# Edge layers of a graph kernel: both one-hots of a group in one VectorE compare with two sources

## The chip, the cores and the metric

The kernel runs on one core of one Trainium2 chip. The metric is the device time of an execution in microseconds; the smaller the better. The core has a matrix engine (TensorE, PE in the profile, its weight loads PEld), VectorE (DVE), ScalarE (ACT), GpSimd (POOL) and SyncE (SP), which mostly issues DMAs. Each engine works through a list of its own and waits on semaphores for the others.

## The reference, cut to what matters

There are 12500 nodes with 128 features and 212500 edges (both directions of 100000 random pairs and a loop at each node), sorted by destination.

```python
def _edge_conv(x, src, dst, W1, b1, W2, b2, n_nodes):
    xi = x[dst]
    xj = x[src]
    m = jnp.concatenate([xi, xj - xi], axis=-1)
    h = jax.nn.relu(m @ W1 + b1) @ W2 + b2
    agg = jax.ops.segment_max(h, dst, num_segments=n_nodes)
    return jnp.where(jnp.isfinite(agg), agg, 0.0)
# three of these with relu between them, then
x = _layernorm(x + edge_layers(x))
# then a relation stage: means of messages over 8 edge types, summed through 8 weight matrices
x = _layernorm(x + relu(relation_stage(x)))
```

## The kernel before

Each of the three edge layers first makes two tables of the nodes: `table` in SBUF (x times W1's first half less its second, plus the bias, looked up by destination) and `tab_b` in DRAM (x times W1's second half, looked up by source). Then it goes over the edges in order of destination. 128 edges are a tile, 4 tiles (GT) are a group of 512 edges, and 8 groups (LG) are the body of a loop. A layer has 428 groups, the three have 1284.

A group goes through the engines like this. The inner function that does a group on each engine is named `step`:

- GpSimd (`gather_body`, L826 to L837) issues four indirect DMAs, one per tile, which fetch the rows of `tab_b` by source into `rows[k]`. It first waits for `s_p1`, which says that TensorE has done with the rows of eight groups before. The list of row numbers of each DMA lies in SBUF (`idx`).
- SyncE loads `two[k]`, the group's local destination numbers (`locs`, bf16, 0 to 255 within a block of 256 nodes, each repeated on all partitions) and the marks at which a new destination begins (`cuts`).
- VectorE (L1556 to L1596) makes the one-hots: `hot_t[s]` is 128 x 2 x 512 f32, with two halves. Half 0 has a one where an edge's local number is the lane's number, half 1 where it is that number plus 128. Two instructions make them, L1562 and L1563, each of 512 columns with one tensor and one number per lane (`pidx`, `pidx_up`). There are two such buffers; VectorE waits in front for `locs` and until TensorE has done with the buffer's former content. The second of the two raises `s_hot`.
- TensorE (L955 to L991) waits for `s_hot`, for the copied part of the table (`s_tabs`), for `s_h1` and for the four gathers (`s_rows`). It adds in PSUM the transposed rows (L966) and the products of the table's two halves with the two one-hots (L968). After that it multiplies by W2 for the group before (L975), and turns the scan's output of two groups before (L990).
- ScalarE applies the relu (L1279), copies the 4 table parts of a later group (L1270) and evicts the turned output (L1291).
- VectorE runs the segment maximum as a scan over the 512 columns (L1590), with `cuts` from SBUF and the product from PSUM as its sources. In its list it comes after the one-hots of two groups later.
- SyncE stores the result in `scan_rows`.

In layer 0 VectorE also makes small one-hots for the segments' ends (L1570 to L1584). In layer 1 it sorts the edges by source and type for the relation stage: pieces of a bitonic sort (`sort_stage`, L1651; L1669, L1670, L1674, L1675) are placed between the groups by a table of times written out by hand. In layer 2 it ranks the sorted keys (L1700 on, among them the scans of L1756 and the RECIPROCAL of L1764). GpSimd's four gathers per group are the same in all three layers. The relation stage after them has gathers of its own (L891).

Ahead of everything VectorE makes small constants (L1412 to L1424), each with a wait for the one before; `pidx` holds the lane's number, `pidx_up` the lane's number plus 128.

Of the kernel before, what the change touches and what calls it, by code (L numbers as in the profile page):

```python
# [32 lines left out]
P = 128  # L33
# [3 lines left out]
GT = 4  # L37
# [8 lines left out]
def gnn_kernel(nc, x, src, dst, etype, params, w_rel, out):  # L46
# [55 lines left out]
    with ExitStack() as ctx:  # L102
        def sb(name, shape, dt=F32):
            return ctx.enter_context(nc.sbuf_tensor(name, shape, dt))
# [9 lines left out]
        ident = sb("ident", [P, P])  # L114
        iota = sb("iota", [P, P])
        pidx = sb("pidx", [P, 1])
        pidx_up = sb("pidx_up", [P, 1])
        lane_f = sb("lane_f", [P, 1])
        ones = sb("ones", [P, 1])
        ones_b = sb("ones_b", [P, 1], BF16)  # L120
# [96 lines left out]
        locs = [v[:, 0:GT * P] for v in two]  # L217
# [13 lines left out]
        hot_t = [a.cut(2 * GT * P).rearrange("p (h e) -> p h e", h=2) for _ in range(2)]  # L231
# [207 lines left out]
        GP_PAD, GP_ALL = 3, 9  # L439
        SLOTS = LG  # L440

        PV_CONST = 13
        PV_FULL = PV_CONST + 2
        PV_WIN0 = PV_FULL + 2
        PV_START = PV_WIN0 + 4
# [734 lines left out]
        def _(act):  # L1180
# [84 lines left out]
            def copy_tables(l, g, s):  # L1265
                _, blk = nc.values_load_multi_w_load_instructions(
                    blocks[0:1, bass.ds(g * GT, GT)], engines=[ACT_ENGINE], min_val=0, max_val=NS,
                    skip_runtime_bounds_check_because=WHY)
                for t in range(GT):
                    last = a_(tabs[s][:, t, :], table[:, bass.ds(blk[t] * W2P, W2P)], ACT.Copy)  # L1270
                last.then_inc(s_tabs, 1)
# [24 lines left out]
            for l in range(3):  # L1296
                if l == 0:
                    act.wait_ge(s_pv, PV_CONST)
                    act.wait_ge(s_w, NW * 16)
# [99 lines left out]
        def _(dve):  # L1399
            v = nc.vector  # L1400
# [3 lines left out]
            def pv(ins):  # L1404

                done[0] += 1
                ins.then_inc(s_pv, 1)
                dve.wait_ge(s_pv, done[0])
                return done[0]
# [10 lines left out]
            pv(v.memset(eps[:, :], EPS))  # L1420
            pv(v.memset(zeros[:, :], 0.0))
            pv(v.tensor_scalar(lane_f[:, :], pidx[:, :], 1.0, None, ALU.add))
            pv(v.tensor_scalar(pidx_up[:, :], pidx[:, :], float(P), None, ALU.add))
            assert pv(v.memset(table[:, NB * P:], 0.0)) == PV_CONST  # L1424

            dve.wait_ge(s_last, 16)
# [129 lines left out]
            def step(l, i, k, lo=False, hi=False):  # L1556
                live = lambda d: not ((lo and k < d) or (hi and k - OV >= d))
                if live(0):
                    at = Lt(l, i, k)
                    dve.wait_ge(s_two[at.k], 16 * (at.n + 1))  # L1560
                    dve.wait_ge(s_p1, at.G - 1 + SLOTS)
                    v.tensor_scalar(hot_t[at.s][:, 0, :], locs[at.k], pidx[:, 0:1], None, ALU.is_equal)  # L1562
                    v.tensor_scalar(hot_t[at.s][:, 1, :], locs[at.k], pidx_up[:, 0:1], None, ALU.is_equal  # L1563
                                    ).then_inc(s_hot, 1)
                    if l == 0:
                        if at.j == 0:
                            dve.wait_ge(s_endc[at.h], 16 * (at.n + 1))
                            dve.wait_ge(s_found, at.G + 1)
                            tick()
                            v.tensor_scalar(end_up, end_c[at.h], float(P), -float(P), ALU.is_ge, ALU.mult  # L1570
                                            ).then_inc(s_lane, 1)
                            for f, side in enumerate((ALU.is_lt, ALU.is_ge)):
                                v.tensor_scalar(lanes[at.h][:, :, f], end_c[at.h], float(P), lane_f[:, 0:1], side, ALU.mult)
                            dve.wait_ge(s_lane, 2 * at.H + 1)
                            tick()
                            v.tensor_tensor(end_lo[at.h], end_c[at.h], end_up, ALU.add).then_inc(s_lane, 1)
                            dve.wait_ge(s_lane, 2 * at.H + 2)
                            tick()
                        dve.wait_ge(s_found, at.G + 1)
                        for t in range(GT):  # L1580
                            col = at.j * GT + t
                            last = v.tensor_scalar(ends[at.s][:, t, :], iota_b[:, :], end_lo[at.h][:, col:col + 1], None,  # L1582
                                                   ALU.is_equal)
                        last.then_inc(s_ends, 1)  # L1584
                if live(2):
                    at = Lt(l, i, k, 2)
                    dve.wait_ge(s_p2, at.G + 3)
                    dve.wait_ge(s_p3, at.G + 1)
                    dve.wait_ge(s_scan, at.G + 2)
                    v.tensor_tensor_scan(scan[at.s], cuts[at.k], ps[:, 2 + at.s, :],  # L1590
                                         scan[1 - at.s][:, GT * P - 1:GT * P], ALU.min, ALU.max).then_inc(s_scan, 1)
                    if l == 0 and at.j == HG - 1:
                        dve.wait_ge(s_found, at.G + 3)
                        tick()
                        v.tensor_copy(end_at[:, :, bass.ds((at.i * 2 + at.h) * HT, HT)],
                                      ps[:, 6 + at.h, 0:2 * HT].rearrange("p (t f) -> p f t", f=2)).then_inc(s_ecol, 1)  # L1596
# [300 lines left out]
            for l in range(3):  # L1897
# [26 lines left out]
                for k in range(LG):  # L1924
                    step(l, 0, k, lo=True)
                alone = (1, SORT_END + 1, WIN_BODY + NQ + 1)[l]
                for i in range(1, alone):
                    for k in range(LG):
                        step(l, i, k)
                        if l == 1:  # L1930
                            sort_work(i, k)
                        else:
                            rank_work(i, k)
                with loop(dve, alone, NL) as i:
                    for k in range(LG):
                        step(l, i, k)
# [163 lines left out]
```

## Time and profile before

| | us |
|---|---|
| median of 3 runs | 9618.12 (9596.58 to 9622.49) |
| profiled execution | 9607.98 |
| its span | 9606.1 |
| edge layers' gathers, first and last start | 145.4 and 7164.9 |
| GpSimd busy | 7060.4 |
| TensorE busy | 6722.9 |
| VectorE busy | 4648.1 |
| ScalarE busy | 4896.4 |

The busy time of an engine is the time in which at least one of its instructions ran. A group of instructions is the instructions of one source line and shape; a mean over it hides that a few are much longer. "Idle before" is time in which the engine had none running just ahead of such an instruction, and behind the arrow stands what ended it. Where that is "issue", nothing of another engine did. In a timeline an instruction stands with its start and its duration.

### The profile page before, as it was taken

To read this page: it belongs to the slowest core of one execution; us is meant where nothing else is said; L and a number is where in the kernel's file an instruction comes from. 1 tells how busy PE (TensorE), PEld (TensorE's weight loads), DVE (VectorE), ACT (ScalarE), POOL (GpSimd) and SP (SyncE) were. 2 spreads that over 40 slices of the span, in tenths; PEclk is the share of its full clock that TensorE was granted. 3 is DMA by queue.
4 is the path that set the end of the run, shared out by engine and by line. 5 is a ranking of instruction groups with operands and counts; after the bars stand their busy time and mean duration, and the time that the engine had idled before them with its cause. 6 is when DMAs were issued, how large, how long until landed. Compare 5 with 4: busy or idle time off the path is not lost. (4 is left out here: it accounts for less than half of the span.)

```text
span 9606.1 us, 159944 instructions
## 1 busy us (share of the span) xinstructions
PE 6722.9 (70%) x41098; PEld 5264.4 (55%) x41098; DVE 4648.1 (48%) x9610; ACT 4896.4 (51%) x11866; POOL 7060.4 (73%) x7196
## 2 busy tenths in 40 slices
PE   6777777876677777777767777778768555555555
PEld 5665656665555666566555656656653343333333
DVE  4555555555466555555435444444446333333334
ACT  2444444443344444444424444444445777777776
POOL 4777777776777777777777777777774777777775
PEclk9999999999899999999989999999999777777777
DMA  5555555654455555565545565556657222222222
GB/s 142 153 153 154 153 153 153 153 155 133 120 149 150 151 149 151 149 149 149 155 120 142 163 156 160 161 154 153 156 142 265 54 54 54 54 54 54 54 54 67
DMA packets 896156, 1259.78 MB, mean 131 GB/s; under 512 B 185847, under 2 KB 601079, under 8 KB 895270
## 3 DMA queue, kind: packets, MB, share of 16 engines
q1 hardware_dynamic: 650494, 784.23, 26.5%
q0 software_dynamic: 230048, 471.99, 21.8%
q10 hardware_dynamic: 15408, 0.88, 0.1%
q8 instruction: 121, 1.98, 0.1%
q14 instruction: 85, 0.70, 0.0%
HBM read 834.14 MB, written 424.01 MB: 131 GB/s over the span
## 5 line engine op out<-in xcount | busy, mean ns | idle before, releaser
L834 POOL DMA_INDIRECT agg<-tab_b,agg x5136 | 5109.6, 995 | 1596.4 <-issue 1523.0
L968 PE MATMUL ps<-tab_a 128*128 128x128 f32 x20544 | 3090.0, 285 | 2.8 <-issue 2.8
L968 PEld LDWEIGHTS ps<-tab_a 128*128 128x128 f32 x20544 | 2883.2, 202 | 3.5 <-issue 3.5
L1590 DVE TENSOR_TENSOR_SCAN agg<-agg,ps 128x512 f32<-128x512 bf16 x1284 | 1639.7, 1277 | 2159.3 <-PE ps L975 2158.2
L966 PE MATMUL ps<-ident,agg 128*128 128x128 f32 x5136 | 1482.7, 289 | 1701.4 <-DMA agg<-tab_b,agg 1577.7
L1279 ACT ACTIVATE agg<-ps 128x512 f32<-128x512 f32 x1284 | 766.6, 597 | 3604.2 <-PE ps L968 3596.7
L891 POOL DMA_INDIRECT work<-z_tab,work x1708 | 1611.7, 944 | 576.1 <-issue 498.3
L1163 PE MATMUL ps<-tab_a,work 128*128 128x256 f32 x3416 | 1231.5, 523 | 912.4 <-DMA work<-z_tab,work 631.1
L966 PEld LDWEIGHTS ps<-ident,agg 128*128 128x128 f32 x5136 | 754.0, 147 | 1936.0 <-issue 1349.2
L1270 ACT ACTIVATE tab_a<-tab_a 128x256 f32 x5136 | 1713.6, 404 | 50.8 <-issue 41.1
L1163 PEld LDWEIGHTS ps<-tab_a,work 128*128 128x128 f32 x3416 | 843.4, 258 | 1300.6 <-DVE tab_a L2035 1107.9
L2035 DVE TENSOR_TENSOR tab_a<-ps,tab_a 128x256 f32 x1708 | 724.3, 424 | 1417.7 <-PE ps L1163 1230.9
L975 PE MATMUL ps<-agg,w 128*128 128x512 f32 x2568 | 1345.1, 606 | 0.0
L1356 ACT ACTIVATE tab_a<-tab_a,work 128x256 f32<-128x256 f32 x1708 | 883.7, 588 | 466.5 <-PE ps L1163 452.8
L990 PEld LDWEIGHTS ps<-ident,agg 128*128 128x128 f32 x5136 | 610.4, 141 | 471.3 <-issue 466.5
L990 PE MATMUL ps<-ident,agg 128*128 128x128 f32 x5136 | 786.2, 276 | 2.4 <-DVE agg L1590 2.3
L1347 ACT ACTIVATE tab_a<-work 128x256 f32<-128x256 f32 x1708 | 727.4, 496 | 61.8 <-ACT tab_a L1356 5.7
L1291 ACT ACTIVATE agg<-ps 128x512 f32<-128x512 f32 x1284 | 738.3, 575 | 15.5 <-PE ps L990 10.6
L1582 DVE TENSOR_SCALAR agg<-iota_b,agg 128x128 bf16<-128x128 bf16 x1712 | 327.6, 280 | 688.1 <-PE ps L982 670.1
L1562 DVE TENSOR_SCALAR tab_a<-agg,pidx 128x512 f32<-128x512 bf16 x1284 | 626.3, 488 | 47.9 <-PE ps L968 45.2
L1563 DVE TENSOR_SCALAR tab_a<-agg,pidx_up 128x512 f32<-128x512 bf16 x1284 | 626.7, 488 | 0.0
L813 POOL DMA_INDIRECT work<-scan_rows,endrow x294 | 287.7, 979 | 194.2 <-issue 99.4
(251 smaller groups left out, 2978.9 us busy)
## 6 DMA issues: line engine op xcount, KB each, us to landing
agg<-row_two SPq DMA_DIRECT2D x1284, 256.0 KB
scan_rows<-agg SPq DMA_DIRECT2D x1284, 256.0 KB
agg<-tab_b,agg POOLq DMA_INDIRECT x5136
z_tab<-tab_a SPq DMA_DIRECT2D x84, 512.0 KB, 3.7
work<-z_tab,work POOLq DMA_INDIRECT x1708, 2.5
tab_b<-work SPq DMA_DIRECT2D x42, 448.0 KB, 3.1
work<-in_x SPq DMA_DIRECT2D x26, 448.0 KB, 5.3
z_tab<-work SPq DMA_DIRECT2D x14, 512.0 KB, 3.9
```

The source lines that it names most:

```text
L834: g.indirect_dma_start(rows[k][:, t, :], None, tab_b, bass.IndirectOffsetOnAxis(ap=idx[at.h][:, at.j * GT + t:at.j * GT + t + 1], axis=0)) ...
L891: g.indirect_dma_start(got[k % LG][:, t, :], None, z_tab, bass.IndirectOffsetOnAxis(ap=meta_of(k, 0, t).bitcast(I32), axis=0)).then_inc(s_ ...
L966: mm(to, rows[at.k][:, t, :], ident[:, :], is_transpose=True, start=True, stop=False)
L968: last = mm(to, tabs[at.s][:, t, h * P:(h + 1) * P], hot_t[at.s][:, h, t * P:(t + 1) * P], start=False, stop=(h == 1))
L975: mm(ps[:, 2 + at.s, :], w2[:, l], h1[at.s], start=True, stop=True).then_inc(s_p2, 1)
L990: last = tr(ps[:, 4 + at.s, t * P:(t + 1) * P], scan[at.s][:, t * P:(t + 1) * P], ident[:, :])
L1163: last = mm(flat[:, to:to + W2P], got[k % LG][:, t, :], hot_r[k % 4][:, t, :], start=True, stop=True)
L1270: last = a_(tabs[s][:, t, :], table[:, bass.ds(blk[t] * W2P, W2P)], ACT.Copy)
L1279: a_(h1[at.s], ps[:, at.s, :], ACT.Relu).then_inc(s_h1, 1)
L1291: a_(h2e[at.s], ps[:, 4 + at.s, :], ACT.Copy).then_inc(s_h2e, 1)
L1356: last = a_(hot_r[k % 4][:, t, :], off_r[k % 2][:, t, :], ACT.Relu, scale=meta_of(k, 3, t), bias=meta_of(k, 2, t))
L1590: v.tensor_tensor_scan(scan[at.s], cuts[at.k], ps[:, 2 + at.s, :], scan[1 - at.s][:, GT * P - 1:GT * P], ALU.min, ALU.max).then_inc(s_scan, 1)
```

## The change

The two compares become one. Its first source is `locs`, read twice over, its second the two columns of a new constant `pidx_two`, each number repeated over 512 columns. The destination and the condition are the same, and so are the waits and the semaphore. The constant `pidx_up` falls away, `pidx_two` takes its place, with one more small instruction among the constants.

```diff
-        pidx_up = sb("pidx_up", [P, 1])
+        pidx_two = sb("pidx_two", [P, 2])
...
-        PV_CONST = 13
+        PV_CONST = 14
...
-            pv(v.tensor_scalar(pidx_up[:, :], pidx[:, :], float(P), None, ALU.add))
+            pv(v.tensor_scalar(pidx_two[:, 1:2], pidx[:, :], float(P), None, ALU.add))
+            pv(v.tensor_copy(pidx_two[:, 0:1], pidx[:, :]))
...
-                    v.tensor_scalar(hot_t[at.s][:, 0, :], locs[at.k], pidx[:, 0:1], None, ALU.is_equal)
-                    v.tensor_scalar(hot_t[at.s][:, 1, :], locs[at.k], pidx_up[:, 0:1], None, ALU.is_equal
+                    v.tensor_tensor(hot_t[at.s], locs[at.k].unsqueeze(1).to_broadcast([P, 2, GT * P]),
+                                    pidx_two[:, :].unsqueeze(2).to_broadcast([P, 2, GT * P]), ALU.is_equal
                                     ).then_inc(s_hot, 1)
```

## Rows read from the trace of the kernel before

**Rows 1.** The page: busy us (share of the span) and instructions of each engine.
```profile
PE 6722.9 (70%) x41098; PEld 5264.4 (55%) x41098; DVE 4648.1 (48%) x9610; ACT 4896.4 (51%) x11866; POOL 7060.4 (73%) x7196
```

**Rows 2.** Waits of GpSimd: us in total, times, longest us.
```profile
POOL agg L834 <- issue: 1523.0, 4895, 16.0
...
POOL agg L834 <- PE ps L968: 51.5, 169, 0.3
```

**Rows 3.** Waits of TensorE.
```profile
PE ps L966 <- DMA agg<-tab_b,agg: 1577.7, 985, 16.8
...
PE ps L966 <- DVE tab_a L1563: 95.3, 62, 6.3
```

**Rows 4.** Waits of VectorE.
```profile
DVE agg L1590 <- PE ps L975: 2158.2, 797, 14.5
```

**Rows 5.** Groups of GpSimd, 200:2200, 3060:4660, 5300:6900 us: busy, mean ns | idle before.
```profile
L834 POOL DMA_INDIRECT agg<-tab_b,agg x1556 | 1527.0, 981 | 474.3 <-issue 451.7 <-PE ps L968 16.5 <-ACT agg L1261 6.1
...
L834 POOL DMA_INDIRECT agg<-tab_b,agg x1212 | 1232.4, 1017 | 369.4 <-issue 355.7 <-ACT agg L1261 7.3 <-PE ps L968 6.4
...
L834 POOL DMA_INDIRECT agg<-tab_b,agg x1241 | 1203.5, 970 | 378.3 <-issue 358.8 <-PE ps L968 13.7 <-ACT agg L1261 5.8
```

**Rows 6.** Instructions of line 834: ns min/median/max, first and last start us.
```profile
L834 POOL DMA_INDIRECT agg<-tab_b,agg x5136: 938/944/5210, 145.4 to 7164.9; - x198
```

**Rows 7.** Timeline of VectorE and GpSimd in layer 0: start us, us, instruction.
```profile
1502.92 0.46 DVE L1562 TENSOR_SCALAR tab_a<-agg,pidx 128x512 f32<-128x512 bf16 x1
...
1503.30 0.48 DVE L1563 TENSOR_SCALAR tab_a<-agg,pidx_up 128x512 f32<-128x512 bf16 x1
...
1503.35 1.24 POOL L834 DMA_INDIRECT agg<-tab_b,agg  x1 [0.30 <-issue]
```

**Rows 8.** Timeline in layer 1, two places of the sort.
```profile
3062.89 1.20 DVE L1674 TENSOR_TENSOR work<-work 128x1024 f32<-128x1024 f32 x1
...
3063.10 1.80 POOL L834 DMA_INDIRECT agg<-tab_b,agg  x1 [0.30 <-ACT agg L1261]
...
3073.56 1.20 DVE L1674 TENSOR_TENSOR work<-work 128x1024 f32<-128x1024 f32 x1
...
3073.97 1.61 POOL L834 DMA_INDIRECT agg<-tab_b,agg  x1 [0.30 <-issue]
```

**Rows 9.** Timeline in layer 1, a gather that began before the sort's compare.
```profile
3121.39 0.94 POOL L834 DMA_INDIRECT agg<-tab_b,agg  x1 [0.30 <-issue]
...
3121.77 1.20 DVE L1674 TENSOR_TENSOR work<-work 128x1024 f32<-128x1024 f32 x1
```

**Rows 10.** Timeline in layer 2, the RECIPROCAL and the first of the gathers that began beside it.
```profile
5189.28 12.93 DVE L1764 RECIPROCAL work<-work 128x2048 f32<-128x2048 f32 x1
...
5190.31 0.94 POOL L834 DMA_INDIRECT agg<-tab_b,agg  x1 [0.30 <-issue]
```

**Rows 11.** Timeline in layer 2, the edge scan and a scan of two SBUF sources.
```profile
5153.22 1.28 DVE L1590 TENSOR_TENSOR_SCAN agg<-agg,ps 128x512 f32<-128x512 bf16 x1 [5.99 <-PE ps L975]
...
5153.35 0.94 POOL L834 DMA_INDIRECT agg<-tab_b,agg  x1 [0.30 <-issue]
...
5154.41 4.46 DVE L1756 TENSOR_TENSOR_SCAN work<-work,ones 128x2048 f32<-128x2048 f32 x1
...
5154.60 5.17 POOL L834 DMA_INDIRECT agg<-tab_b,agg  x1 [0.30 <-issue]
```

**Rows 12.** Groups of the page, the first of the two one-hots: busy, mean ns | idle before.
```profile
L1562 DVE TENSOR_SCALAR tab_a<-agg,pidx 128x512 f32<-128x512 bf16 x1284 | 626.3, 488 | 47.9 <-PE ps L968 45.2
```

**Rows 13.** Groups of VectorE, 3060:4660 us.
```profile
L1674 DVE TENSOR_TENSOR work<-work 128x1024 f32<-128x1024 f32 x116 | 139.3, 1201 | 0.0
```

**Rows 14.** Instructions of line 1685, a product with a repeated mask: ns min/median/max.
```profile
L1685 DVE TENSOR_TENSOR work<-ps,work x28: 664/665/668, 3180.2 to 4476.7; 128x512 f32<-128x512 f32 x28
```

**Rows 15.** Timeline of VectorE among the constants.
```profile
6.78 0.15 DVE L1423 TENSOR_SCALAR pidx_up<-pidx 128x1 f32<-128x1 f32 x1
7.05 0.27 DVE L1424 MEMSET tab_a<- 128x256 f32 x1
```

## The prediction

> **What bounds the kernel now.** I read the engines' shares first. GpSimd (POOL) is the busiest at 73%, TensorE 70%, VectorE 48% [rows 1]. Three quarters of the span are edge layers, so what counts is which engine never rests there. The waits of GpSimd say it: ahead of its 5136 row gathers (L834) it waited 1523.0 us for "issue" in 4895 cases, and only 51.5 us for TensorE [rows 2]. "Issue" is time in which nothing outside held it, about 0.30 us ahead of every gather. It is simply working through its list. The other engines wait for it: TensorE 1577.7 us for the gathers' landings against 95.3 us for the one-hots [rows 3], and VectorE 2158.2 us for TensorE ahead of its scan [rows 4].
>
> The second step is whether the length of a gather is the length of a group. In layer 0, 1556 gathers fell into 2000 us, one per 1.285 us; that is the mean gather, 0.981, and 474.3 / 1556 = 0.305 of idle. In the part of layer 1 that holds the sort's long compares, 1212 fell into 1600 us, one per 1.320 us: 1.017 and 0.305 again [rows 5]. So nanoseconds added to a gather come out in the period one for one. A group is four gathers and there are 1284 groups: 0.1 us per group is 128 us of the kernel.
>
> The third step is why a gather is longer in one place than in another. Its median is 0.944 us, its longest 5.210 us [rows 6]. The timelines of GpSimd and VectorE side by side show it. A gather that began 0.05 us into the second one-hot compare took 1.24 us, not 0.94 [rows 7]. Beside the sort's TENSOR_TENSOR, which has two sources in SBUF, gathers that began 0.21 and 0.41 us into it took 1.80 and 1.61 us [rows 8]. Put e for the end of the VectorE instruction and s for the start of the gather: 0.94 + (e - s - 0.13) gives 1.24 for the first, 1.80 and 1.60 for the others. The gather needs something that VectorE holds, once, some 0.1 us after its start, and waits for it to the end of that instruction. One that is past this point isn't disturbed: at 3121.39 a gather was already 0.38 us old when the same TENSOR_TENSOR began; it took 0.94 us, and the TENSOR_TENSOR its usual 1.20 [rows 9]. What decides isn't VectorE's being busy: beside a 12.93 us RECIPROCAL (one source) the ten gathers that began kept 0.94 us; one stands here [rows 10]. Neither does the scan of L1590, whose second source lies in PSUM: the gather at 5153.35 began inside one and took 0.94 us. Beside a scan of two SBUF sources, the second a column of ones repeated 2048 times, a gather took 5.17 us [rows 11].
>
> **The change, part by part.**
>
> *The compare itself.* Removed per group: two TENSOR_SCALAR of 512 columns, 488 ns each (the second's mean is the same), 0.98 us [rows 12]. Added: one TENSOR_TENSOR of 1024 columns from SBUF to SBUF. The trace has that shape in the sort: 1201 ns for one of its two lines [rows 13]; I take 1.20 us. Two things differ from these rows. One source is bf16, and both are repeated by a step of zero. The nearest row on repeating, 512 columns with a repeated mask at 665 ns [rows 14], shows no cost. From that row's pace 1024 columns would be 1.33 us at most, and from the two compares removed at least 0.98. So VectorE is busy some 0.22 us more per group (bounds 0 and +0.35). It idles 2158.2 / 1284 = 1.68 us per group for the scan's input [rows 4], and that covers it. If this cover were gone, it would be 0.22 x 1284 = 280 us. The one-hots come ready about 0.33 us later (0.38 + 0.48 from start to end now [rows 7]); TensorE was kept by them 62 times [rows 3], so at most 62 x 0.33 = 20 us are added to its wait, in a TensorE that has over a microsecond per group to spare. I count nothing.
>
> *What it does to the gathers.* This is the term. The new instruction has two sources in SBUF, like the sort's compares and the scan with the ones, and it lasts 1.20 us in one piece. A gather starts each 0.94 + 0.30 = 1.24 us, so nearly every one-hot finds one gather at its sensitive point. If the two run free of each other, the wait per group is 1.17 x 1.17 / (2 x 1.24) = 0.55 us, with 1.17 = 1.20 - 0.03 as the stretch that is held. The trace has a dose to check this by: in the sort window a gather averaged 1017 ns, in the quieter part of layer 2 970 ns [rows 5]; 1212 x 0.047 = 57 us over 116 pairs of these compares is 0.49 us per pair. In a pair, the gather caught in the first half passes at the seam, and its successor needs its turn about 1.14 us later, near the end of the second, so a pair costs about what one does. I take 0.50. Bounds: 0.25 (the 0.49 split evenly over the pair's two instructions), and 1.17 (every one catches a gather at its very start).
>
> *What goes.* The old compares also hold gathers up. In layer 2, where little else runs on VectorE, the mean gather is 970 ns [rows 5] against the median of 944 [rows 6]: 4 x 0.026 = 0.10 us per group. Layer 0, with its other small compares, has 4 x 0.037 = 0.15. I take 0.12.
>
> *Net:* 0.50 - 0.12 = 0.38 us per group, x 1284 = 488 us. Bounds 0.13 x 1284 = +167 and 1.05 x 1284 = +1348.
>
> *Preparation.* One more tiny instruction, with its own wait, before the first layer: from L1423's start to the next instruction's is 0.27 us [rows 15]. It stands in a chain that GpSimd waits for, so +0.3 us.
>
> The Trainium skill has a rule here ("SBUF — State Buffer", section "SBUF: two separate sides"): VectorE and GpSimd share a pair of ports under an exclusive lock, which a VectorE instruction in a two-port mode takes, and one with two SBUF inputs too, against a GpSimd instruction that reads SBUF. That speaks against this change, and rows 8 and 11 agree with it. But it also says that whoever starts first keeps the pair for the whole instruction; rows 9 show otherwise for these gathers. What that would give is rival B.
>
> **Sum.** The profiled execution took 9607.98 us (span 9606.1). 9608 + 488 = 10096 us; I say 10100. The median of the runs, 9618.12, is 0.1% above the profiled one, which is within this. Layers alone change; the relation stage (L891) has none of these compares.
>
> **Rivals.**
>
> *A, the other side: the new compare does not hold the gathers.* Place: the sensitive point of L834. Its lane numbers are two values per partition, repeated, and might be held inside VectorE, as a scalar is. Then the old stalls go and nothing replaces them: -0.12 x 1284 = -154 us, 9454 us. It decides if the mean gather falls to about 945 ns. For it: the scan with its second source in PSUM is harmless. Against it: the repeated ones of rows 11 were no protection. 8%.
>
> *B, whole instructions exclude each other.* Then the compare would wait for the running gather, start with its end, and the next gather, 0.30 us later, would stand for 1.20 - 0.30 = 0.90 us in each group: +0.78 x 1284 = 1002, 10610 us. This is the skill's rule as written; rows 9 speak against it. 3%.
>
> *C, the phases fall well.* The compare starts when a scan ends, which follows from a gather's landing, so its phase is not random. If it mostly began just after a gather's sensitive point, the stall would be near the lower bound or under it: +167 us at 0.25, 9775 us; down to no change. The old compares bear on this: by the same random reckoning their two holds of about 0.45 us would cost 2 x 0.45 x 0.45 / 2.48 = 0.16, and layer 2 shows 0.10. 9%, 2% of it within no change.
>
> *D, the compare is slow.* At the pace of the two-source scan of rows 11 (4.46 us for 2048 columns) it would last 2.2 us, and hold a gather 2.2 - 0.62 = 1.6 us in each group: +1.48 x 1284 = 1900, 11510 us. 2%; no compare in the trace is that slow.
>
> **How the numbers follow.** The forecast has 78%, with its own range from 0.32 to 0.52 us net per group, 10020 to 10280 us. Below it lie A and C, above B and D and the three-in-a-row of layer 1 (sort, sort, one-hot), which can catch two gathers. For 8 in 10 I give 9950 to 10320. A difference of 0.3%, 29 us, is about what can be told from none; by that: faster 0.09, same 0.02, slower 0.89.
>
> **What would show it.** One group L1563 of TENSOR_TENSOR 128x1024 with 1284 instructions near 1200 ns; mean of L834 up from 995 to about 1090 ns (0.38 / 4), its median still near 944 in the undisturbed ones, and gathers of up to 2.1 us lying beside the compare by the formula above; the idle of GpSimd still "issue" at 0.30; TensorE's wait for landings larger; relation stage unchanged. It is wrong if L834 keeps its mean, or if the mean rises and the span doesn't.

## The result and the profile after

The changed kernel took 10176.36 us in the median of 4 runs (10153.47 to 10189.58), the kernel before 9620.31 on the same chip. The ratio is 1.0579, with a 95% interval of 1.0551 to 1.0607: slower by 5.8%. A later job gave 10173.92 against 9603.69, ratio 1.0592 (1.0574 to 1.0610). There are chips on which the kernel before takes a third longer and the sign turns; they have a section below.

The page of the changed kernel, engines and the groups that answer to [rows 1] and [rows 12]:

```profile
PE 6930.3 (68%) x41098; PEld 5462.9 (54%) x41098; DVE 5043.6 (50%) x8327; ACT 4899.5 (48%) x11866; POOL 7631.3 (75%) x7196
...
L834 POOL DMA_INDIRECT agg<-tab_b,agg x5136 | 5673.4, 1105 | 1596.0 <-issue 1566.4
...
L891 POOL DMA_INDIRECT work<-z_tab,work x1708 | 1615.7, 946 | 576.3 <-issue 499.5
...
L1563 DVE TENSOR_TENSOR tab_a<-agg,pidx_two 128x1024 f32<-128x1024 bf16 x1284 | 1547.7, 1205 | 44.2 <-PE ps L968 44.0
```

The gathers of the kernel before, whole trace:

```profile
L834 POOL DMA_INDIRECT agg<-tab_b,agg x5136 | 5109.6, 995 | 1596.4 <-issue 1523.0
```

The span grew from 9606.1 to 10180.4 us, by 574.3. The gathers' busy time grew by 5673.4 - 5109.6 = 563.8 us, and the idle time ahead of them stayed, 1596.0 against 1596.4. The relation stage's gathers (L891) gained 1615.7 - 1611.7 = 4 us. Longer gathers in the edge layers account for 98% of the loss. The compare takes 1205 ns in the mean.

The answers to [rows 3] and [rows 4], waits of TensorE and VectorE:

```profile
PE ps L966 <- DMA agg<-tab_b,agg: 1924.9, 955, 17.0
...
PE ps L966 <- DVE tab_a L1563: 107.4, 53, 8.7
```
```profile
DVE agg L1591 <- PE ps L975: 2299.2, 781, 16.9
```

TensorE waits 347 us longer for landings and 12 us longer for the one-hots. VectorE is busy 395 us longer and yet waits 141 us longer for TensorE: the other engines stand behind GpSimd. The answers to [rows 5], in layer 0, in the sort's stretch of layer 1 (3255 to 5055 us here) and in the quiet part of layer 2 (5700 to 7500):

```profile
L834 POOL DMA_INDIRECT agg<-tab_b,agg x1444 | 1560.8, 1081 | 440.3 <-issue 431.8 <-PE ps L968 4.6 <-ACT agg L1261 4.0
...
L834 POOL DMA_INDIRECT agg<-tab_b,agg x1219 | 1429.9, 1173 | 371.7 <-issue 364.7 <-ACT agg L1261 5.2 <-PE ps L968 1.8
...
L834 POOL DMA_INDIRECT agg<-tab_b,agg x1288 | 1386.2, 1076 | 392.8 <-issue 385.4 <-ACT agg L1261 4.0 <-PE ps L968 3.4
```

Per group that is 4 x (1081 - 981) = 0.40 us more in layer 0, 4 x (1173 - 1017) = 0.62 among the sort, 4 x (1076 - 970) = 0.42 in layer 2. The timeline of layer 0 has the single case, to be read like [rows 7]:

```profile
1506.13 1.20 DVE L1563 TENSOR_TENSOR tab_a<-agg,pidx_two 128x1024 f32<-128x1024 bf16 x1
1506.20 1.95 POOL L834 DMA_INDIRECT agg<-tab_b,agg  x1 [0.30 <-issue]
...
1509.24 1.21 DVE L1563 TENSOR_TENSOR tab_a<-agg,pidx_two 128x1024 f32<-128x1024 bf16 x1
1509.71 1.56 POOL L834 DMA_INDIRECT agg<-tab_b,agg  x1 [0.31 <-issue]
```

The prediction's formula, 0.94 + (e - s - 0.13), gives 1.94 and 1.55 us. It holds for the whole trace and not only here: of the gathers that start while a compare runs, between 0.03 us after its start and 0.16 us before its end, there are 1000, and all 1000 took what the formula says, within 0.07 us. Among the sort, where three two-source instructions follow each other without a pause, two gathers in a row are caught:

```profile
3269.17 1.20 DVE L1675 TENSOR_TENSOR work<-work 128x1024 f32<-128x1024 f32 x1
3269.52 1.67 POOL L834 DMA_INDIRECT agg<-tab_b,agg  x1 [0.30 <-issue]
3270.29 1.22 DVE L1676 TENSOR_TENSOR work<-work 128x1024 f32<-128x1024 f32 x1
3271.42 1.22 DVE L1563 TENSOR_TENSOR tab_a<-agg,pidx_two 128x1024 f32<-128x1024 bf16 x1
3271.49 1.97 POOL L834 DMA_INDIRECT agg<-tab_b,agg  x1 [0.30 <-issue]
```

### The profile page after: what moved, and what is told of

Read it like the earlier page. It is cut to its first block and busy times, and to the rows that moved or that the text cites. A ratio compares the mean times of both kernels' runs of the same rounds, so it can differ in the third digit from the quotient of the medians.

```text
span 10180.4 us, 158661 instructions
## 1 busy us (share of the span) xinstructions
PE 6930.3 (68%) x41098; PEld 5462.9 (54%) x41098; DVE 5043.6 (50%) x8327; ACT 4899.5 (48%) x11866; POOL 7631.3 (75%) x7196
## 5 line engine op out<-in xcount | busy, mean ns | idle before, releaser
L834 POOL DMA_INDIRECT agg<-tab_b,agg x5136 | 5673.4, 1105 | 1596.0 <-issue 1566.4
L968 PE MATMUL ps<-tab_a 128*128 128x128 f32 x20544 | 3273.4, 295 | 8.3 <-issue 8.3
L968 PEld LDWEIGHTS ps<-tab_a 128*128 128x128 f32 x20544 | 3047.4, 213 | 9.2 <-issue 9.2
L966 PE MATMUL ps<-ident,agg 128*128 128x128 f32 x5136 | 1534.0, 299 | 2051.0 <-DMA agg<-tab_b,agg 1924.9
L891 POOL DMA_INDIRECT work<-z_tab,work x1708 | 1615.7, 946 | 576.3 <-issue 499.5
L966 PEld LDWEIGHTS ps<-ident,agg 128*128 128x128 f32 x5136 | 783.4, 153 | 2279.5 <-issue 1573.8
L1563 DVE TENSOR_TENSOR tab_a<-agg,pidx_two 128x1024 f32<-128x1024 bf16 x1284 | 1547.7, 1205 | 44.2 <-PE ps L968 44.0
L975 PE MATMUL ps<-agg,w 128*128 128x512 f32 x2568 | 1374.5, 618 | 0.0
L990 PEld LDWEIGHTS ps<-ident,agg 128*128 128x128 f32 x5136 | 612.6, 142 | 483.6 <-issue 478.8
L990 PE MATMUL ps<-ident,agg 128*128 128x128 f32 x5136 | 786.4, 276 | 2.4 <-DVE agg L1591 2.3
L975 PEld LDWEIGHTS ps<-agg,w 128*128 128x128 f32 x2568 | 419.2, 205 | 0.0
```

Of the source, the lines that this page charges most:

```text
L834: g.indirect_dma_start(rows[k][:, t, :], None, tab_b, bass.IndirectOffsetOnAxis(ap=idx[at.h][:, at.j * GT + t:at.j * GT + t + 1], axis=0)) ...
L891: g.indirect_dma_start(got[k % LG][:, t, :], None, z_tab, bass.IndirectOffsetOnAxis(ap=meta_of(k, 0, t).bitcast(I32), axis=0)).then_inc(s_ ...
L966: mm(to, rows[at.k][:, t, :], ident[:, :], is_transpose=True, start=True, stop=False)
L968: last = mm(to, tabs[at.s][:, t, h * P:(h + 1) * P], hot_t[at.s][:, h, t * P:(t + 1) * P], start=False, stop=(h == 1))
L975: mm(ps[:, 2 + at.s, :], w2[:, l], h1[at.s], start=True, stop=True).then_inc(s_p2, 1)
L990: last = tr(ps[:, 4 + at.s, t * P:(t + 1) * P], scan[at.s][:, t * P:(t + 1) * P], ident[:, :])
```

## The experiments

Twelve runs, in four jobs of one chip each; the two jobs with 13110.83 and 13109.51 had the same chip. Each job ran the kernel before too, and only ratios within a job are compared. The edits are against the changed kernel, that of one_source_sum against the kernel before; "again" and "third" are the same kernel on another occasion.

| run | its time | kernel before there | ratio (95%) | mean gather, ns |
|---|---|---|---|---|
| changed_again | 10173.92 | 9603.69 | 1.0592 (1.0574 to 1.0610) | 1100 |
| one_source_sum_again | 9468.79 | 9603.69 | 0.9857 (0.9841 to 0.9874) | 966 |
| one_source_sum | 13332.94 | 13110.83 | 1.0174 (1.0150 to 1.0198) | 958 |
| two_of_512 | 12494.4 | 13110.83 | 0.9531 (0.9495 to 0.9566) | 1046 |
| one_source_1024 | 12836.09 | 13110.83 | 0.9800 (0.9773 to 0.9826) | 992 |
| lanes_in_psum | 12650.78 (1 run) | 13110.83 | | 1067 |
| two_of_512_again | 12475.43 | 13109.51 | 0.9508 (0.9477 to 0.9540) | 1049 |
| one_source_1024_again | 12856.89 | 13109.51 | 0.9802 (0.9751 to 0.9853) | 994 |
| lanes_in_psum_again | 12633.26 (1 run) | 13109.51 | | 1058 |
| two_of_512_third | 12234.58 | 12867.11 | 0.9508 (0.9485 to 0.9531) | 1050 |
| one_source_1024_third | 12674.27 | 12867.11 | 0.9826 (0.9791 to 0.9862) | 993 |
| changed_third | 12372.54 | 12867.11 | 0.9595 (0.9555 to 0.9635) | 1082 |

**The second source, moved to PSUM.** This is the run that tells a second SBUF source from a long instruction. The instruction is the same; in the last 192 groups of layer 2 its lane numbers come from two free columns of a PSUM bank. A small copy ahead of them, not shown in this cut, puts the numbers there.

```diff
+                    of = ps[:, 7, 0:2] if lanes_in_psum else pidx_two[:, :]
                     v.tensor_tensor(hot_t[at.s], locs[at.k].unsqueeze(1).to_broadcast([P, 2, GT * P]),
-                                    pidx_two[:, :].unsqueeze(2).to_broadcast([P, 2, GT * P]), ALU.is_equal
+                                    of.unsqueeze(2).to_broadcast([P, 2, GT * P]), ALU.is_equal
```

> The changed kernel, but in the last 196 groups or so of layer 2 the lane numbers of the compare lie in PSUM and not in SBUF. Same instruction, same columns, same output; 1.2 to 1.3 us long. Theory (the second SBUF source is what holds the gathers): in that stretch no gather is stretched by the compare, the mean of line 834 falls from about 1085 ns to 944 to 950, and the kernel is about 0.5 x 192 = 96 us shorter than the changed one, 10080 us. Rival (a VectorE instruction of this length holds the gathers wherever its sources lie; or it's the writing to SBUF that does): mean near 1085 ns, 10180 us.

> The changed kernel with the lane numbers in PSUM for the last 192 groups of layer 2, again. Theory: in that stretch the mean gather is 944 to 950 ns where the changed kernel has about 1085, and the kernel takes 0.5 x 192 = 96 us less than the changed one, near 10080 us. Rival: no difference in the stretch, 10170.

Of lanes_in_psum_again, the compares of both kinds (all instructions of the line: ns min/median/max), then GpSimd's gathers in the stretch before the move (7000 to 8360 us) and in the one after it (8370 to 9790):

```profile
L1565 DVE TENSOR_TENSOR tab_a<-agg,pidx_two x1092: 1160/1201/1273, 144.5 to 9810.4; 128x1024 f32<-128x1024 bf16 x182
L1565 DVE TENSOR_TENSOR tab_a<-agg,ps x192: 1193/1196/1220, 8366.3 to 9789.5; 128x1024 f32<-128x1024 bf16 x192
```
```profile
L835 POOL DMA_INDIRECT agg<-tab_b,agg x773 | 814.4, 1054 | 499.6 <-ACT agg L1262 261.8 <-issue 226.0 <-PE ps L969 11.8
...
L835 POOL DMA_INDIRECT agg<-tab_b,agg x764 | 720.7, 943 | 707.4 <-ACT agg L1262 482.2 <-issue 224.3 <-PE ps L969 0.9
```

And its timeline inside the second stretch, VectorE and GpSimd:

```profile
8416.43 1.20 DVE L1565 TENSOR_TENSOR tab_a<-agg,ps 128x1024 f32<-128x1024 bf16 x1
...
8416.93 0.94 POOL L835 DMA_INDIRECT agg<-tab_b,agg  x1 [0.30 <-issue]
```

The compare is as long (1196 ns), writes the same place, and no longer touches a gather: 943 ns in the mean, where the same kernel had 1054 just before. By the formula the gather at 8416.93 would have taken 0.94 + 0.57 = 1.51 us. 96 gathers of this stretch start while such a compare runs, and none of them is lengthened. One difference between the two stretches is not the source: up to the move VectorE also ranks the keys of layer 2. The same last 192 groups with the numbers in SBUF settle it. In changed_third they have a mean of 1054 ns with gathers of up to 1978 ns, with the numbers in PSUM the longest of the 768 takes 962 ns:

```profile
L834 POOL DMA_INDIRECT agg<-tab_b,agg x768 | 809.4, 1054 | 537.4 <-ACT agg L1261 304.0 <-issue 227.8 <-PE ps L968 5.6
```
```profile
L835 POOL DMA_INDIRECT agg<-tab_b,agg x768: 938/944/962, 8370.3 to 9794.1; - x192
```

So neither the length of the VectorE instruction nor its writing holds the gathers, but its second source in SBUF. The expected 96 us in the whole time could not be tested: the changed kernel did not run on this chip, which is of the kind whose time does not follow the gathers (see below).

**One source, kept slow.** The old compares have one source and still hold gathers up. If what they hold is what a second source holds, a form of theirs that keeps off it should be harmless. The Trainium skill ("SBUF — State Buffer", section "Who interferes with whom") excepts the tensor_scalar form that also writes out its accumulator from those that enter the two-port modes. The cut leaves out the allocation of `hot_sum`.

```diff
-                    v.tensor_scalar(hot_t[at.s][:, 0, :], locs[at.k], pidx[:, 0:1], None, ALU.is_equal)
-                    v.tensor_scalar(hot_t[at.s][:, 1, :], locs[at.k], pidx_up[:, 0:1], None, ALU.is_equal
-                                    ).then_inc(s_hot, 1)
+                    v.tensor_scalar(hot_t[at.s][:, 0, :], locs[at.k], pidx[:, 0:1], 0.0, ALU.is_equal, ALU.add,
+                                    accum_out=hot_sum[:, 2 * at.s:2 * at.s + 1])
+                    v.tensor_scalar(hot_t[at.s][:, 1, :], locs[at.k], pidx_up[:, 0:1], 0.0, ALU.is_equal, ALU.add,
+                                    accum_out=hot_sum[:, 2 * at.s + 1:2 * at.s + 2]).then_inc(s_hot, 1)
```

> The kernel before, with both compares of 512 columns also adding up their output into a spare column per lane (which nothing reads). The result of the compare is unchanged. The Trainium skill ('SBUF - State Buffer', 'Who interferes with whom') says that this form stays out of the two-port modes, which would make the compare slower, and harmless to GpSimd; no row yet shows it. Theory (what holds the gathers is the second port, by a second source or a faster mode): each compare takes 0.6 us or more instead of 0.46, yet gathers fall to 945 to 955 ns from 995, and the kernel to 9440 to 9500 us, below both others. Rival 1 (a longer VectorE instruction holds gathers longer, whatever its sources): 0.6 us each, some 0.3 us per group, 9800 us. Rival 2 (the form changes nothing): 9610 us.

> The kernel before with both compares also adding up their output, again. Where the kernel before takes about 9620 us: theory (what holds the gathers is VectorE's second port; the mean gather was 958 ns in the first run of this kernel) expects 9440 to 9500 us; rival (nothing is gained from shorter gathers) 9610. Where it takes 13100: 1.7% above the kernel before, as in the first run.

The page of one_source_sum_again, engines and groups, and a piece of its timeline:

```profile
PE 6686.9 (71%) x41098; PEld 5231.8 (55%) x41098; DVE 5294.9 (56%) x12178; ACT 4894.8 (52%) x11866; POOL 6915.1 (73%) x7196
...
L835 POOL DMA_INDIRECT agg<-tab_b,agg x5136 | 4963.7, 966 | 1596.1 <-issue 1520.8
...
L1563 DVE TENSOR_SCALAR_CACHE_REDUCE tab_a<-agg,pidx 128x512 f32<-128x512 bf16 x1284 | 931.2, 725 | 40.9 <-PE ps L969 40.7
L1565 DVE TENSOR_SCALAR_CACHE_REDUCE tab_a<-agg,pidx_up 128x512 f32<-128x512 bf16 x1284 | 951.1, 741 | 0.0
```
```profile
1506.48 0.74 DVE L1565 TENSOR_SCALAR_CACHE_REDUCE tab_a<-agg,pidx_up 128x512 f32<-128x512 bf16 x1
1506.61 0.94 POOL L835 DMA_INDIRECT agg<-tab_b,agg  x1 [0.30 <-issue]
```

VectorE now spends 1.47 us per group on the one-hots, half as much again as before and more than in the changed kernel, and the kernel is the fastest of all: 9468.79 us, 1.4% below the kernel before (the 95% interval, 0.9841 to 0.9874, is clear of 1) and within the expected 9440 to 9500. A gather that falls into the compare keeps its 0.94 us: 1063 start while one runs, by the same count as above, and none is lengthened. The gathers' busy time fell by 5109.6 - 4963.7 = 145.9 us and the span by 9606.1 - 9465.0 = 141.1. The prediction's 0.12 us per group for the old compares was thus real (154 us by its reckoning), and the trace agrees with what the Trainium skill says of this form, as far as its effect on GpSimd goes; the ports themselves no trace shows. In layer 0 (200 to 2200 us) the mean gather is 945 ns, so the rest of the 966 comes from the work of layers 1 and 2:

```profile
L835 POOL DMA_INDIRECT agg<-tab_b,agg x1601 | 1512.2, 945 | 488.0 <-issue 461.8 <-ACT agg L1262 14.6 <-PE ps L969 11.6
```

**Shorter holds, and one long one-source instruction.** These two vary the length and the kind of the instruction that a gather meets. The second leaves out the plus 128, so its second half is a copy of the first and it computes something else.

```diff
-                    v.tensor_tensor(hot_t[at.s], locs[at.k].unsqueeze(1).to_broadcast([P, 2, GT * P]),
-                                    pidx_two[:, :].unsqueeze(2).to_broadcast([P, 2, GT * P]), ALU.is_equal
-                                    ).then_inc(s_hot, 1)
+                    for h in range(2):
+                        last = v.tensor_tensor(hot_t[at.s][:, h, :], locs[at.k],
+                                               pidx_two[:, h:h + 1].to_broadcast([P, GT * P]), ALU.is_equal)
+                    last.then_inc(s_hot, 1)
```
```diff
-                    v.tensor_tensor(hot_t[at.s], locs[at.k].unsqueeze(1).to_broadcast([P, 2, GT * P]),
-                                    pidx_two[:, :].unsqueeze(2).to_broadcast([P, 2, GT * P]), ALU.is_equal
-                                    ).then_inc(s_hot, 1)
+                    v.tensor_scalar(hot_t[at.s], locs[at.k].unsqueeze(1).to_broadcast([P, 2, GT * P]),
+                                    pidx[:, 0:1], None, ALU.is_equal).then_inc(s_hot, 1)
```

> The changed kernel with its one-hots made by two TENSOR_TENSOR of 512 columns, each still with two sources in SBUF. VectorE works longer than in the changed kernel (the sort's compares of this shape take 0.68 us each, so some 1.33 us per group against 1.20). Theory (a gather waits at one point of its own, some 0.1 us after its start, to the end of the two-source instruction it meets): two holds of about 0.64 us with a seam between them cost 2 x 0.64 x 0.64 / 2.48 = 0.33 us per group where one of 1.17 costs 0.55, so the mean gather of layer 0 falls from 1080 ns to about 1025 and the kernel to about 9880 us (9800 to 9960). Rival (what costs is VectorE's time, or its later one-hots): no better than the changed kernel, 10180 us or a little more.

> Two TENSOR_TENSOR of 512 columns, again, for the case that the kernel before takes about 9610 us here. Theory: 0.33 us per group at the gathers where the single one costs 0.55, mean gather of layer 0 near 1025 ns, kernel near 9880 us (9800 to 9960). Rival (VectorE's time counts, 1.33 us per group against 1.20): 10180 us or more.

> Two TENSOR_TENSOR of 512 columns, for a chip on which the kernel before takes about 9610 us. Theory (length of one hold counts): near 9880 us (9800 to 9960), mean gather of layer 0 near 1025 ns. What speaks against my size: where the kernel before takes 13110 us, layer 0's mean was 1078 and 1081 ns with these, as with the single compare (1080), and only layers 1 and 2 had less (1060 and 1000). If that holds here, about 10000 us. Rival (VectorE's time): 10180 us or more.

> The one-hots in one instruction of 1024 columns with one source and one number per lane. It leaves out the plus 128 of the second half, which becomes a copy of the first. It separates the merging from the second source. Duration some 0.73 us (the old compare of 512 takes 0.46, and half of that is there whatever the columns are). Theory (every hold counts by its length, a one-source compare's too): a hold of 0.70 us costs 0.70 x 0.70 / 2.48 = 0.20 us per group at the gather's first point, and up to 0.1 at the later one that the old compares show, so 0.20 to 0.30 where the old compares cost 0.12: 9720 to 9840 us. Rival 1 (only a second source holds gathers up for long): mean gather as before, 9610 us. Rival 2 (one-source compares this long get through like the RECIPROCAL): gathers at 945 ns, 9460 us.

> One instruction of 1024 columns with one source (the plus 128 of the second half left out), again. In its first run it took 0.73 us or so; theory: 9720 to 9840 us by the length of the hold; rival (one hold of 0.7 is no worse than two of 0.45): 9610.

> One instruction of 1024 columns with one source, plus 128 left out, for a chip on which the kernel before takes about 9610 us. Theory by the square of the hold: 9720 to 9840 us. Rival (merging one-source compares is no loss; where the kernel before takes 13110 us, the mean gathers were 991, 1005, 979 ns against 982, 1017, 986 of the kernel before): 9600 us.

None of these met a chip of the first kind, so their expected times stand untested; what can be read is their gathers. In the job of the third runs the two compares of 512 columns (median 0.681 us each) left the mean gather at 1050 ns and the single one at 1082, 0.42 and 0.55 us per group above the 944 of undisturbed ones. That difference of 0.13, where I expected 0.22, isn't evidence for the rule: it comes from layers 1 and 2 alone. In layer 0 (200 to 3000 us), where neither the sort nor the ranking runs, the order is the other way, two_of_512_third first, then changed_third:

```profile
L834 POOL DMA_INDIRECT agg<-tab_b,agg x1627 | 1760.9, 1082 | 1039.5 <-ACT agg L1261 548.2 <-issue 473.1 <-PE ps L968 11.4
```
```profile
L834 POOL DMA_INDIRECT agg<-tab_b,agg x1554 | 1606.6, 1034 | 1194.2 <-ACT agg L1261 734.1 <-issue 455.8 <-PE ps L968 3.0
```

The traces show one thing that the expectation had wrong. It let a gather caught by the first compare pass at the seam between the two. In two_of_512_third, 615 gathers were due in the first compare; 307 went on at its end, but 249 waited to the end of the second (the rest, at the edges, did not wait), and the other two runs of this kernel have about the same shares. One of them, 0.42 us into the pair, took 0.94 + (1506.27 - 1505.42 - 0.13) = 1.66 us by the end of the second:

```profile
1505.00 1.27 DVE L1564 TENSOR_TENSOR tab_a<-agg,pidx_two 128x512 f32<-128x512 bf16 x2
...
1505.42 1.67 POOL L834 DMA_INDIRECT agg<-tab_b,agg  x1 [0.30 <-issue]
```

In the pairs of the sort (L1674 and L1675 of the kernel before) all 98 held gathers passed at the seam. Why half of them don't here is open, and so is what the length of one hold is worth.

The one-source compare of 1024 columns (median 0.729 us) left 993 ns, no more than the two old compares have on the first chip (995). So merging as such did no harm to the gathers, and my square rule, which wanted 0.20 to 0.30 us per group, gave too much; rival 1 of that run is nearer. Its trace also shows that such a compare catches gathers at a second point. Of 183 gathers that had started 0.15 to 0.50 us before it, 179 were lengthened, by the formula with 0.83 in place of 0.13; here 0.94 + (507.15 - 506.11 - 0.83) = 1.15:

```profile
506.11 1.16 POOL L834 DMA_INDIRECT agg<-tab_b,agg  x1 [0.30 <-issue]
506.42 0.73 DVE L1563 TENSOR_SCALAR tab_a<-agg,pidx 128x1024 f32<-128x1024 bf16 x1
```

The two-source compare has no such point: of 237 gathers that had started 0.15 to 0.50 us before one in the changed kernel, 2 were lengthened.

**The changed kernel as a control.**

> The changed kernel itself, as the control that the first four runs lacked: on their chip the kernel before took 13111 us and not 9618. In those traces TensorE gets its instructions one at a time, about 0.7 us apart, in part of every loop body, which the trace of before hasn't. Where the kernel before takes about 9620 us, both theories expect 10180. Where it takes about 13100: theory (TensorE's slow stretches bound the kernel there, and get shorter the slower the gathers come) expects the changed kernel below the kernel before, near 12500; rival (the gathers' stalls add up on any bound) 13600.

> The changed kernel, as the control of this job. Where the kernel before takes 9610 us: 10175 us. Where it takes 13110 us: theory (in stretches TensorE gets its instructions about 0.7 us apart, and these stretches get shorter the slower the gathers come) below the kernel before, near 12500 us; rival (stalls of the gathers add up on any bound) 13600 us.

On the first kind of chip it repeated its time to 0.03%. On the other it came out below the kernel before, near the expected 12500 us, which the next section is about.

## The chips on which the sign turns

On two chips the kernel before took 12867 to 13111 us. On the one of 12867 the changed kernel ran too, and it was faster, by 4% (0.9595); on the other only its variants ran. Waits of GpSimd in changed_third, then the groups of TensorE in its layer 0 (200 to 3000 us), then the same first group on the first chip (the changed kernel, 200 to 2200 us):

```profile
POOL agg L834 <- ACT agg L1261: 1854.7, 186, 20.7
POOL agg L834 <- issue: 1549.8, 4914, 17.5
```
```profile
L968 PE MATMUL ps<-tab_a 128*128 128x128 f32 x6217 | 1137.7, 309 | 390.1 <-issue 385.4
```
```profile
L968 PE MATMUL ps<-tab_a 128*128 128x128 f32 x5776 | 906.4, 292 | 0.0
```

GpSimd is no longer without rest: 186 times it waits, up to 20.7 us, until ScalarE has copied a loop body's row numbers, which ScalarE does after a wait for TensorE. TensorE has idle time ahead of its products for which the profile shows no releaser, 385 us where the first chip has none. In such a stretch of changed_third the weight loads come one by one:

```profile
1509.66 0.18 PEld L966 LDWEIGHTS ps<-ident,agg 128*128 128x128 f32 x1 [0.70 <-issue]
1510.10 0.29 PEld L968 LDWEIGHTS ps<-tab_a 128*128 128x128 f32 x1 [0.25 <-issue]
1512.22 0.29 PEld L968 LDWEIGHTS ps<-tab_a 128*128 128x128 f32 x1 [1.83 <-issue]
```

Where nothing stops them, four loads of L968 take 0.53 us together (1.00 us at the lower clock: in the changed kernel on the first chip at 1509.96 us, with a granted clock of 0.51). In the stretch above it was 0.50, so the lower clock explains the 0.29 us of a load but not the 1.83 us between two of them.

So I read the bound there as TensorE's supply of instructions in certain stretches, with the gathers' stalls in the slack; no run varied that supply. The gathers are stalled there as elsewhere (1082 ns). Two more differences stand beside it. The granted clock over layer 0 was 0.76 in changed_third and 0.95 on the first chip; the products were longer for it, 309 against 292 ns, about 106 us over the 6217 of them, against 390 us of idle time ahead of them. Whether the clock is lower because TensorE idles or for a reason of its own isn't separated. And the relation stage, which has none of the compares, is longer there too: from the start of the last edge gather to the end of the span 2799 us against 2446.

Why the changed kernel is ahead is open. My theory was that the stretches get shorter the slower the gathers come. The control came out on its side (0.9595, not the rival's rise), and so did the kernel with the quickest gathers, the slowest of all (1.0174). Two variants speak against it, at least in part. Two compares of 512 have shorter gathers than the single one (1050 against 1082 ns) and are ahead of it (0.9508); by layer, from the first gather's start to the last's, the theory fails in layer 1 (2909 us with 1065 ns against 2984 with 1145) and holds in layers 0 and 2 (2941 with 1083 against 3058 with 1035, 3031 with 1003 against 2998 with 1066). And the one-source compare of 1024 columns has gathers as short as the old compares' on the first chip (993 against 995) and is still 2% ahead of the kernel before (0.98, 0.9802, 0.9826). What makes these chips differ was not tried.

## Why the prediction was right

- *What bounds the kernel.* GpSimd's list of gathers, one for one with the span: 563.8 of 574.3 us. This holds where the kernel before takes about 9610 us.
- *The compare.* 1.20 us taken, 1.205 measured. VectorE was busy 395.5 / 1284 = 0.31 us per group longer, not 0.22: the two old compares overlapped by some 0.1 us [rows 7], which a sum of durations leaves out. No cost of it shows in the time, as predicted. Of the later one-hots nothing was taken; TensorE's wait for them grew by 12 us of the 20 allowed.
- *The stall.* 0.38 us net per group taken, 563.8 / 1284 = 0.44 measured. In layers 0 and 2 it is 0.40 and 0.42. The size was short in the sort's stretch: 0.62 over 1219 / 4 = 305 groups, 73 us more than 0.38 gives. That is most of the 86 us between the forecast's 488 and the 574.3; the remaining groups of layer 1 gave some of it back. There the compare follows two of the sort's two-source instructions with no pause, which I had named as what can catch two gathers but had left out of the sum. Free-running phases (0.55, less 0.12, 0.43) would have been nearer than the 0.50 taken after the sort's dose (0.49): the gathers held at the formula's point by the new compare lost 687 us, 0.53 per group. The 0.50 rests on an assumption for pairs that the trace bears out (98 of 98 passed at the seam), but a dose taken as the difference of two stretches' means carries whatever else differs between them.
- *What goes.* The 0.12 us of the old compares: shown by one_source_sum_again, 145.9 / 1284 = 0.11. That they also catch gathers at a second point wasn't seen; it was in the measured means, so the term didn't suffer.
- *Rival A* (repeated numbers don't count as a source) and *rival B* (whole instructions exclude each other) fell: gathers were held, and by the formula for one point. *C* and *D* did not occur; against *C* the prediction had a guess of 9% and no derivation, so part of hitting the range is luck.
- That the second SBUF source is the cause was argued from rows 8, 10 and 11 before; lanes_in_psum_again shows it, on a chip of the other kind. That the stall costs time one for one is shown on the first kind, where gathers and span grew together and, in one_source_sum_again, shrank together.

Not foreseen was that the answer depends on the chip. The bound was read from one trace, and another chip has another bound.

## What to carry to other kernels

When an engine that starts indirect gathers never rests, read the length of one gather against what VectorE is doing at its start: a VectorE instruction with two SBUF sources that is running 0.1 us after the gather's start stretches it to its own end, and so do the fast one-source compares of this kernel, which catch it at a second point as well. The slower form that also adds up its output stretched none. One two-source VectorE instruction in place of two one-source ones was then a loss even though VectorE had time, and more VectorE time was a gain. Put the second source in PSUM (shown for the gathers, not for the whole time), or pick the slower form, and test on more than one chip, since a bound elsewhere can turn the sign.

## What the runs showed that was not expected

The lane numbers in PSUM made a compare with neither a cost in time (1196 against 1201 ns) nor one to GpSimd. Adding an output sum to a compare made it 0.725 us where it had been 0.488, and the kernel 1.4% faster. The Trainium skill ("SBUF — State Buffer", section "Who interferes with whom") says of tensor_tensor with both inputs in SBUF that it contends with GpSimd's reads, but also that it was not seen to stall DMAs, from which it infers that descriptor generation wants the write side. For these gathers, which take their row numbers from SBUF, the first holds and the second does not: one starting just inside the compare takes 1.95 us against 0.94. And one program's time differed by 34 to 37% between chips (9603.69 against 12867.11 and 13110.83), with the ratio of the two kernels at 1.0592 on one and 0.9595 on another.
